# Mixture-of-experts decoder layer: routed results kept in sorted order and gathered, instead of scattered to tokens and reloaded

## The reference, cut to what matters

```
x = layernorm(x + self_attention(x))              # x is 32 x 64 x 128
x = layernorm(x + cross_attention(x, ctx))
weights = softmax(x @ gW + gb)                    # 15 experts
topv, topi = top_k(weights, 3)                    # 3 experts for each of 2048 tokens
shared = gelu(x @ sW1 + sb1) @ sW2 + sb2          # hidden 512, every token
routed = sum over the 3 of topv * (gelu(x @ rW1[e] + rb1[e]) @ rW2[e] + rb2[e])   # hidden 256
return layernorm(x + shared + routed + x)
```

## Time and profile before

| what | value |
|---|---|
| median of 3 runs | 285.67 us |
| lowest, highest | 283.55, 286.89 us |
| span of the profiled execution | 319.6 us |
| the profiled execution's own time | the page gives none beside the span |
| PE, DVE, ACT, POOL busy | 75%, 69%, 60%, 56% of the span |
| granted TensorE clock, mean | 0.936 of full |
| scatters of results by POOL (L2047) | 62, from 212.4 to 313.2 us |
| scatters of tokens by POOL (L1986) | 48, from 118.4 to 199.6 us |

### The profile page before, as it was taken

How to read it: one execution, slowest core, us unless ns; L and a number is a source line. 1 busy time by engine, 2 the same in 40 slices (tenths; PEclk the granted TensorE clock), 3 DMA queues, 4 the chain that set the end, 5 groups by cost and what they waited for, 6 DMA issues and landing times.

```text
span 319.6 us, 7117 instructions
## 1 busy us (share of the span) xinstructions
PE 241.1 (75%) x2283; PEld 179.8 (56%) x2283; DVE 221.6 (69%) x630; ACT 192.2 (60%) x423; POOL 179.0 (56%) x166
## 2 busy tenths in 40 slices
PE   6989989877988767996761299688868867785970
PEld 3676868655535434452451156586857757674960
DVE  6777999989999998998520497043444434856875
ACT  4697997549976976754470350344554546563665
POOL 6132755330666738985677467135656566665752
PEclk9999999999997998998978589799999999999778
DMA  7672830124000002952211133123132263354462
GB/s 218 217 213 46 181 128 2 37 67 133 2 0 2 0 4 62 378 215 49 86 58 50 44 101 108 41 61 101 53 99 76 75 187 90 91 168 123 150 185 90
DMA packets 38597, 31.89 MB, mean 100 GB/s; under 512 B 12864, under 2 KB 31552, under 8 KB 38432
## 3 DMA queue, kind: packets, MB, share of 16 engines
q1 hardware_dynamic: 34608, 23.90, 26.6%
q0 software_dynamic: 3520, 7.27, 6.7%
q10 hardware_dynamic: 432, 0.27, 0.3%
HBM read 19.95 MB, written 11.47 MB: 98 GB/s over the span
## 4 chain that ended last, share of the span: by engine, by line
PE 44%; DVE 27%; issue 14%; ACT 4%; another core or an unknown queue 4%; POOL 4%; DMA 1%; DVEq 0%; SPq 0%; ACTq 0%
PE psum L994 12%; PE psum L985 9%; PE psum L783 5%; DVE prob_sums L1496 4%; PE psum L763 4%; DVE maxes L1490 3%; PE psum L977 2%; PE psum L568 2%; DVE prob_sums L1410 2%; POOL x_srt L1986 2%; PE psum L585 1%; DMA xT<-x_t 1%; DVE turned_room L1421 1%; DVE maxes L1405 1%
## 5 line engine op out<-in xcount | busy, mean ns | idle before, releaser
L2047 POOL DMA_INDIRECT y_tok<-k_heads,y_rows x62 | 62.7, 1012 | 50.8 <-ACT k_heads L1327 34.4
L1319 ACT ACTIVATE k_heads<-psum,k_heads 128x128 f32<-128x128 f32 x124 | 38.7, 365 | 38.5 <-PE psum L985 33.6
L1986 POOL DMA_INDIRECT x_srt<-v_blocks,slot x48 | 48.0, 1000 | 21.3 <-issue 17.2
L994 PE MATMUL psum<-k_heads 128*128 128x128 f32 x248 | 42.4, 295 | 18.0 <-issue 12.1
L1823 DVE COPY k_heads<-psum 128x128 f32<-128x128 f32 x62 | 17.8, 289 | 48.9 <-PE psum L977 32.7
L994 PEld LDWEIGHTS psum<-k_heads 128*128 128x128 f32 x248 | 34.2, 200 | 21.9 <-issue 15.2
L985 PE MATMUL psum<-k_heads 128*128 128x128 f32 x248 | 40.6, 288 | 5.2 <-DVE k_heads L1823 4.2
L1963 POOL TENSOR_TENSOR k_heads<-k_heads,inv_sums 128x1024 f32<-128x1024 f32 x14 | 27.1, 1939 | 24.0 <-DVE inv_sums L1503 23.9
L985 PEld LDWEIGHTS psum<-k_heads 128*128 128x128 f32 x248 | 33.8, 198 | 8.5 <-DVE k_heads L1823 7.4
L1951 POOL TENSOR_TENSOR probs<-probs,inv_sums 128x512 f32<-128x512 f32 x16 | 16.8, 1050 | 28.9 <-DVE inv_sums L1415 28.7
L1327 ACT ACTIVATE k_heads<-psum,k_heads 128x128 f32<-128x128 f32 x62 | 22.9, 370 | 11.3 <-PE psum L994 9.1
(11 more groups left out here) (191 smaller groups left out, 530.1 us busy)
## 6 DMA issues: line engine op xcount, KB each, us to landing
expert_w<-e_w SPq DMA_DIRECT2D x1, 4369.0 KB
k_heads<-x_srt SPq DMA_DIRECT2D x62, 65.0 KB
q_heads<-y_tok SPq DMA_DIRECT2D x8, 256.0 KB
x_srt<-pad SPq DMA_DIRECT2D x16, 65.0 KB
xT<-x_t SPq DMA_DIRECT2D x4, 256.0 KB, 5.1
ctxT_k<-ctx_k SPq DMA_DIRECT2D x2, 512.0 KB, 5.5
v_scr<-v_rows SPq DMA_DIRECT2D x4, 256.0 KB, 2.8
ctxT_v<-ctx_v SPq DMA_DIRECT2D x2, 512.0 KB, 5.0
```

Of the source, the lines that this page charges most:

```text
L994: mm = pe.matmul(bank[6 + t % 2][:, 0:E], h_tile[:, t % 2, a, :], tile_weights(t)[:, FE + E * a:FE + E * a + E], start=(a == 0), stop=(a = ...
L1319: ins = act.activation(h_tile[:, t % 2, a, :], bank[2 + t % 2][:, P * a:P * a + P], ACT.Gelu, bias=tile_weights(t)[:, EW - 2 + a:EW - 1 + a])
L1986: pool.indirect_dma_start(out=x_srt, out_offset=bass.IndirectOffsetOnAxis(ap=slot[:, n:n + 1], axis=0), in_=payloads[:, g, k, :], in_offse ...
L2047: pool.indirect_dma_start(out=y_tok, out_offset=bass.IndirectOffsetOnAxis(ap=y_rows[:, t:t + 1].bitcast(mybir.dt.uint32), axis=0), in_=y_t ...
```

## The change

- A routed result is stored in the order in which it is computed. SP writes each `y_tile` with a plain DMA of 128 rows to `y_srt`, a DRAM table of 32-bit integers with the same row order as `x_srt` (the float bits are copied as they are).
- POOL's 62 scatters of results are gone. When the stores of the tiles that a chunk needs have landed, POOL gathers the chunk's results straight into SBUF: 12 indirect DMAs for a chunk, 48 in all, at the row numbers in `slot` that the dispatch used.
- The counts of tiles to wait for are now four rows (one for a chunk), read by POOL (16 reads); SP reads 4 counts before the loop instead of 8, and none in it. SP reads the row table once for loads and once for stores.
- The gate is no part of a row any more (rows are 128 numbers) and ACT no longer scales by it; it is multiplied in DVE's final sums, with one instruction for each group and pick: 48 instead of 12. ACT's copies for the second and third pick, and DVE's `tile_rows`, are gone.
- The sums of chunks 0 and 1 stand at tiles 42 and 57 of the loop; those of chunks 2 and 3 stand behind it. The last chunk is summed group by group. All output stores stand behind the loop.
- The last chunk's pieces of the shared expert move to tiles 21, 24, 27 and 30.
- The padding of 128 rows at the end of `x_srt` is written earlier.

```diff
-        SUMS_AT = (39, 48, 57)
-        ROOTS_AT = 52
-        SHARED_TILES = (8, 14, 20, 26)
+        SUMS_AT = (42, 57)
+        SHARED_TILES = (21, 24, 27, 30)
...
+            def y_stored(t, rows):
+                sp.wait_ge(s_y_tile, t + 1)
+                if t >= NY:
+                    sp.wait_ge(s_y_stored[t % NY], 16 * (t // NY))
+                sp.dma_start(y_srt[bass.ds(rows[t % 4], P), :], y_tile[:, t % NB, :].bitcast(I32)).then_inc(s_y_stored[t % NY], 16)
+
+            for t in range(NB):
+                if t % 4 == 0:
+                    x_rows_at = x_row_of(t)
+                x_loaded(t, x_rows_at)
             for t in range(NT):
+                if t + NB < NT:
+                    if t % 4 == 0:
+                        x_rows_at = x_row_of(t + NB)
+                    sp.wait_ge(s_tile_turned, t + 1)
+                    x_loaded(t + NB, x_rows_at)
                 if t % 4 == 0:
-                    row_of = nc.values_load_multi_w_load_instructions(
...
+                    y_rows_at = row_of(t)
+                y_stored(t, y_rows_at)
...
-            def payload(c):
-                act.wait_ge(s_x2, 4 * c + 4)
-                for k in range(1, TOPK):
-                    act.copy(payloads[:, 4 * c:4 * c + 4, k, 0:E], x2[:, 4 * c:4 * c + 4, :]).then_inc(s_payloads, 1)
...
-                        act.wait_ge(s_y_scattered[t % NB], 16 * (t // NB))
-                    act.activation(y_tile[:, t % NB, :], bank[6 + t % 2][:, 0:E], ACT.Copy,
-                                   scale=x_tile[:, t % NB, E:E + 1]).then_inc(s_y_tile, 1)
+                        act.wait_ge(s_y_stored[t % NY], 16 * ((t - NB) // NY + 1))
+                    act.copy(y_tile[:, t % NB, :], bank[6 + t % 2][:, 0:E]).then_inc(s_y_tile, 1)
...
+            def added_last(j):
+                g = 4 * (NC - 1) + j
+                dve.wait_ge(s_y_last[j], 16 * TOPK)
+                for k in range(TOPK):
+                    routed(dve.scalar_tensor_tensor(out=acc[:, g, :], in0=routed_y[k][:, g, :], scalar=gate_cols[:, g, k:k + 1],
+                                                    in1=acc[:, g, :], op0=ALU.mult, op1=ALU.add))
+                routed(dve.bn_stats(bn3[:, g, :], acc[:, g, :]))
+                dve.bn_aggr(mean_var3[:, g, :], bn3[:, g, :]).then_inc(s_y_sum, 1)
...
-            for t in range(NT):
-                pool.wait_ge(s_y_tile, t + 1)
-                pool.wait_ge(s_y_rows, t // 4 + 1)
-                pool.indirect_dma_start(out=y_tok, out_offset=bass.IndirectOffsetOnAxis(
-                    ap=y_rows[:, t:t + 1].bitcast(mybir.dt.uint32), axis=0),
-                    in_=y_tile[:, t % NB, :], in_offset=None).then_inc(s_y_scattered[t % NB], 16)
+            pool.wait_ge(s_landed, 1)
+            landed = [[pool.value_load(t_landed[0:1, c, k:k + 1], ...) for k in range(NY)] for c in range(NC)]
+            for c in range(NC):
+                for k in range(NY):
+                    pool.wait_ge(s_y_stored[k], landed[c][k])
+                pool.sem_inc(s_y_through, 1)
+                for n in range(4 * TOPK * c, 4 * TOPK * (c + 1)):
+                    g, k = n // TOPK, n % TOPK
+                    pool.indirect_dma_start(out=routed_y[k][:, g, :].bitcast(I32), out_offset=None, in_=y_srt,
+                                            in_offset=bass.IndirectOffsetOnAxis(ap=slot[:, n:n + 1], axis=0)
+                                            ).then_inc(s_y_got[c] if c < NC - 1 else s_y_last[g % 4], 16)
```

More of the change, by code:

```diff
@@ L70 @@
 RUNS = NL * NE
-DONE_BY = tuple((4 * P * TOPK * (c + 1) + NE * (P - 1)) // P for c in range(NC))
 SOON = (NC - 1) * 4 * TOPK
 NB = 8
+NY = 4
 NS = 5
-XW = E + 2
-ROWS = NE * ROOM + P
+LATE = 4
+ROWS = NE * ROOM + TABLE * P
 K_IOTA, K_BASE, K_T, K_TP, K_J = 0, NE, 2 * NE, 2 * NE + TABLE, 2 * NE + 2 * TABLE
@@ L462, in _ @@
             sp.wait_ge(s_scattered, 16 * (SOON - 1))
-            for t in range(NT):
-                if t % 4 == 0:
-                    row_of = nc.values_load_multi_w_load_instructions(
[L466 to L489, removed]
@@ L490, in _, with row_of @@
-            for g in range(4):
-                sp.wait_ge(s_final_v, g + 1)
-                store(sp, 0, g)
-            for k in range(NB):
-                sp.wait_ge(s_y_scattered[k], landed_all[k])
-            reload_y(sp, NC - 1)
-            for g in range(4):
-                sp.wait_ge(s_final, g + 1)
-                store(sp, 1, g)
-            for g in range(4):
-                sp.wait_ge(s_final, 5 + g)
-                store(sp, NC - 2, g)
-            for g in range(2):
-                sp.wait_ge(s_final_v, 5 + g)
+            def row_of(t):
+                return nc.values_load_multi_w_load_instructions(
+                    tile_of(t, 0), engines=[SP], min_val=0, max_val=ROWS - P,
+                    skip_runtime_bounds_check_because="the table ends at the last tile's row")[1]
@@ new lines, in x_row_of, with x_loaded @@
+            def x_row_of(t):
+                return nc.values_load_multi_w_load_instructions(
+                    tile_of(t, 2), engines=[SP], min_val=0, max_val=NE * ROOM,
+                    skip_runtime_bounds_check_because="the table ends at the last tile's row")[1]
+            def x_loaded(t, rows):
+                if t < 4 * LATE:
+                    if t % 4 == 0:
+                        sp.wait_ge(s_late_rows, rows_of[t // 4])
+                elif t == 4 * LATE:
+                    sp.wait_ge(s_late_rows, late_rows)
+                sp.dma_start(x_tile[:, t % NB, :], x_srt[bass.ds(rows[t % 4], P), :]).then_inc(s_x_tile[t % NB], 16)
@@ L504, in _ @@
+            for c in range(NC - 1):
+                for g in range(4):
+                    sp.wait_ge(s_final, 4 * c + g + 1)
+                    store(sp, c, g)
+            for g in range(2):
+                sp.wait_ge(s_final_v, g + 1)
                 store(sp, NC - 1, g)
@@ L1252, in _ @@
             exps2(8)
-            payload(0)
             q_masked2(3, range(0, 2))
@@ L1277, in _ @@
             u2_out(13)
-            payload(1)
             exp_logits(1)
@@ L1827, in tiles_landed @@
             def tiles_landed():
-                routed(dve.tensor_copy(done_count[:, :], more_sum[0:1, NL - 1:NL + 1, NE - 1]))
-                for n in range(2):
-                    routed(dve.tensor_scalar(used_f[:, :], row_consts[0:1, K_T:K_T + TABLE], done_count[:, n:n + 1], 16.0,
-                                             ALU.is_lt, ALU.mult))
-                    with nc.allow_low_precision(reason="whole numbers below 2**24"):
-                        ins = dve.tensor_reduce(t_landed[0:1, n, :], used_f[:, :].rearrange("p (j k) -> p k j", k=NB), AX_X, ALU.add)
-                    if n == 0:
-                        routed(ins)
@@ L1920, in _ @@
                     expert_of = expert_staged(t + 2, expert_of)
+            root_seed(0, NC - 2)
+            for n in range(3):
+                root_newton(0, NC - 2)
+            sum_mean(0, NC - 2)
+            for k in range(TOPK):
+                added(NC - 2, k)
+            sum_stats(NC - 2)
             root_seed(NC - 2, NC - 1)
@@ L1926, in _ @@
             sum_mean(NC - 2, NC - 1)
-            added(NC - 1, 0)
-            added(NC - 1, 1)
-            added(NC - 1, 2)
-            sum_stats(NC - 1)
+            dve.wait_ge(s_acc, NC)
+            for j in range(4):
+                added_last(j)
+            last_stats()
             dve.wait_ge(s_rstd3, 1)
```

146 lines of the change are left out of this document (56 added, 90 removed).

## The result

| | median, us | lowest to highest | runs |
|---|---|---|---|
| before | 285.85 | 283.55 to 286.89 | 4 |
| after | 297.51 | 294.89 to 299.36 | 4 |

The ratio is 1.042, 95% interval 1.036 to 1.048: 11.7 us slower, where 6.3 were forecast (292.0, range 276 to 301).

The account below looks back on a forecast made before the run. SP's pace of 1.25 us a tile, then POOL's chain of gathers, was to set the end: 95.7 us behind the first result against 88.2, so 285.67 + 7.5 - 1.0 = 292.2 us, range 276 to 301.

Parts of the forecast that it names:

- 1.25 a tile: Tile loop of the changed kernel: SP's issuing of loads and stores sets the pace, between 1.16 and 1.32 us a tile.
- Two rows of twelve gathers: POOL behind the loop: chunk 3's gathers follow chunk 2's without a gap, 15.1 us a chunk at 1.26 each.
- From the last gather to the end: Tail: last data landing 1.3 us, last group's sums 1.2, unchanged rest 5.4; together 7.9 us.
- 88.2: Kernel before: us from first result to end in timed runs, 285.67 less 197.5, the first profile's 212.1 without 14.6 of holes.
- The edits costed at nothing: Gates in sums, ACT copies, row collecting, moved shared expert pieces, earlier padding, POOL's count reads: each covered, 0 us.
- the time at which chunk 2 is whole: In the loop: chunk 2's results stored and ready to gather 57.6 us behind the first result.
- slower still: Rival: loop at 1.35 us a tile, stores costing SP 0.66, loop before at POOL's pace; 301 us; chance 0.15.
- The gain ahead of the loop: Before the first tile: SP reads four counts fewer, 1.7 us, of which 1.0 was counted.
- Close to POOL's pace: Loop of the kernel before: timed runs go at about POOL's scatter pace, about 1.3 us a tile.
- no change: Rival: loop at PE's 1.0 us a tile, a gather 1.26, gather chain as long as scatter chain; 285.5 us; chance 0.21.
- a gain: Rival "faster": SP's issue overlaps, loop at PE's 1.0 us a tile, a gather 0.96; 274 us; chance 0.22.
- One cover: DVE's sums: dearer gate multiply-adds, 13.4 instead of 8.2 us, hidden by loop and last gathers; 2.6 us without the latter cover.

Follow-up runs that it names:

- before_again: The kernel before, profiled once more with no edit, since its first profile was 34 us longer than its timed runs: 282.5 us, span 280.6.
- before_fewer_counts: The kernel before, with SP reading two counts of late rows ahead of the loop instead of eight: 286.3 us, ratio 1.004.
- half_stores: The changed kernel, with SP issuing only the even tiles' stores and the gathers reading token rows in place of results: 288.9 us, ratio 1.019.
- half_scatters: The kernel before, with POOL scattering only the even tiles' results and the chunk reloads reading other rows of the same size: 283.8 us, ratio 0.999.
- few_gathers: The changed kernel with only the first pick's gathers, 4 for a chunk instead of 12, added three times in the sums: 292.2 us, ratio 1.032.
- early_gathers: The changed kernel, with all 48 gathers waiting only for the first eight stores and reading token rows in place of results: 290.3 us, ratio 1.020.

## Why the prediction was right, and where its sizes were off

**The mechanism of the changed kernel held.** SP sets the loop's pace: 1.25 a tile was forecast, 1.27 stands in the steady stretch, and SP waits no more for results. Two rows of twelve gathers back to back ahead of DVE's last sums, 1.25 us each: 30.2 us forecast for chunks 2 and 3, 30.9 measured (256.81 to 287.69). From the last gather to the end 7.9 forecast, 8.4 measured. The time of the kernel before from its first result to the end, inferred as 88.2 from the disturbed execution, is 87.0 in the undisturbed one. That this came so near is partly luck: the first result was put 3.9 us too late (197.5, measured 193.6), and the end 5.1 us, because the median of the timed runs (285.67) stood in for a span (280.6 in an execution timed at 282.5). The edits costed at nothing that were tried (the shared expert's place) cost nothing that can be seen.

**The mis-sized term is the time at which chunk 2 is whole.** Forecast 57.6 us behind the first result, measured 256.81 - 189.4 = 67.4. The term was 44 tiles at 1.25 and 2.6 of landing. SP's steady pace gives 44 x 1.27 = 55.9; the store of tile 44 was issued 63.8 us behind the first. The missing 7.9 us are stops of SP that a steady pace leaves out: 2.1 for the last token scatters (above), and four issues that took 1.3 to 1.95 us in place of 0.35, 4.7 us together; two of them (the last section has what went on beside them):

```profile
221.09 1.38 SPq L462 DMA_DIRECT2D k_heads<-x_srt  x1
...
233.77 1.95 SPq L462 DMA_DIRECT2D k_heads<-x_srt  x1
```

The rest is small gaps. Landing and POOL's wake-up took 3.5 instead of 2.6. Together with the gathers and the tail the end came 106.7 us behind the first result, not 95.7: 11.0 too little. Over the whole loop a tile took 81.7 / 61 = 1.34, the pace of the rival "slower still" (1.35), and its 301 came nearer to the measured 297.5 than the forecast's 292; but its reason, a dearer store, is not what happened: a store costs SP what a load costs, 0.55, and the stops made the difference.

**The gain ahead of the loop was undersized, for a reason that is only partly shown.** 1.0 was forecast, the first result came 4.2 us earlier. What the fewer counts give can be read: from SP's last padding to its first load of a tile 5.6 us pass in before_again, 3.3 in after and 3.0 in before_fewer_counts, so 2.3. The rest is not of the counts: SP's padding of the experts' rows begins at 172.7 in before_again and at 170.2 in after, and over the nine profiles of the changed kernel and its versions at 168.2 to 173.4, so that the first result comes anywhere from 187.5 to 192.6. The counts alone gave the kernel before nothing, since its loop then waits for POOL's token scatters. The changed kernel meets that wait too (2.1 us), but four tiles later, because it reads counts for tiles up to 15.

Forecast 7.5 - 1.0; measured between the profiles 11.0 + 7.5 + 1.2 (the kernel before is 87.0, not 88.2) - 4.2 = 15.5.

**The reasoning on the kernel before was right on a number and wrong on a cause.** "Close to POOL's pace" is true of its rows; that POOL leaving the loop would leave PE at 1.0 was not. The rivals of no change and of a gain rested on that 1.0, and half_stores shows 1.2; half_scatters shows that POOL's leaving frees nothing. They were given 0.43 of the chance between them, more than they deserved.

**One cover was told too lightly.** DVE's sums of chunk 2 "lie under the last gathers; without that cover 2.6 us". That prices only the dearer multiply-adds. What lies there is 16.3 us of sums and roots, where the kernel before has 6.3: chunk 2's sums and the roots of chunks 0 and 1 stood in the loop before and were put at nothing. While the gathers are late this costs little, but it keeps any repair of the gathers from paying more than 3 to 7 us (few_gathers, early_gathers).

## What to carry to other kernels

A scatter finishes its work as each tile is done; a gather of the same rows can start only when the last of its sources is stored. Comparing their counts and prices misses this: 48 gathers in place of 62 scatters saved POOL 18 us of work (14 at 1.26), and the stretch behind the loop grew by 16.6. When a full engine is to be relieved, halve its work first and look whether the time moves; here (half_scatters) it would have said that there was nothing to gain. And a tail is often several chains of one length: early gathers gave 7 us, early gathers with the sums in the loop 13.

## What the runs showed of the hardware that was not expected

Single issues of a plain DMA by SP took 1.3 to 1.95 us where the median is 0.33 to 0.36, four times in 64 us of the loop. The gathers are not what they have in common: two of the four (191.67, 203.79) come before the first gather (219.12), and few_gathers, with 16 gathers instead of 48, has four long issues as well, 3.3 us over the median in place of 4.7. What they have in common stands in the DMA view: beside each of the four, one packet of 16 KB is moved for a queue that the page calls "instruction". For the stretches 191.6 to 193.2 and 233.7 to 235.8:

```profile
q8 instruction: 1, 0.02, 4.3%
```

```profile
q8 instruction: 1, 0.02, 4.5%
```

Between these moments (193.2 to 203.4, 205.1 to 221.0, 222.5 to 233.7) the queue has no packet. The whole loop of after has six such packets, and the six issues of SP over 0.6 us are the ones beside them. Over the nine profiles of the changed kernel and its versions 45 of 46 issues of a tile's load or store over 0.6 us overlap a packet of that queue. That the packets lengthen the issues, and for which engine they are fetched, no run shows.
